# A batch pipeline of SSD mixer and selected-token block: inputs of the next batch normalised inside the scan, gating on one engine, softmax ahead of the decay parts, index sum in bf16

## The chip, the cores and the metric

The kernel runs on 1 core of one Trainium2 chip. The metric is the device time of one launch in microseconds (us). Three runs of the kernel before took 1541.77 to 1546.73 us, median 1543.58 us. One further run was profiled; every row below is from it.

## The reference

Input x is 8 batches of 1024 tokens by 256. Each batch goes through a modulated mixer (a selective state-space scan with 8 heads, state 64, inner width 512) and then a modulated block that works on the 127 tokens with the highest router weights only.

```python
h = _layernorm(x) * (1 + ca) + sa
x = x + ga * mixer(h)
h = _layernorm(x) * (1 + cb) + sb
x = x + gb * block(h)

# mixer
x = silu(causal_conv(h @ Wx.T)); z = h @ Wz.T
b = x @ Wb.T; c = x @ Wc.T; dt = softplus(x @ Wdt.T + b_dt)
state = exp(dt * a) * state + (dt * b) x ;  y = c . state        # per token, per head
y = y + d * x
yn = (y - mean) / sqrt(var + eps) * gn_w + gn_b                  # mean, var over tokens and channels of a head
mixer = (yn * silu(z)) @ Wout.T

# block
weights = h @ router_w + router_b ; sel = sorted indices of the top 127
q, k, v = rope(rmsnorm(h[sel]) @ wq) ... ; a = softmax(q k / 4 + mask[sel, sel])
x1 = h[sel] + (a v) @ wo ; x2 = x1 + gelu(rmsnorm(x1) @ w1) @ w2
block = h for all tokens but sel ; x2 * weights[sel] there
```

## The kernel before

The program is written out by hand: each engine (TensorE = PE, VectorE = DVE, ScalarE = ACT, GpSimd = POOL, SyncE = SP for transfers) has its own list of instructions, works them in order, and waits on semaphores. Nothing reorders them.

PE's `batch(b, f)` interleaves the projections of batch b with the block of batch f = b - 1 and ends with `scan(b)`. So there are 8 passes: batch 0 alone, seven passes with a block of the batch before, and a **tail** in which the block of batch 7 runs alone. A pass on PE goes: transposes of the normalised input (`ln_in`, two halves, line L1509), `x_proj` and `z_proj` (L1521), the output projection of batch f (`out_`, L1685), the projections to B and C (`bc_proj`, L1521), with the steps of the block between them (`ffn_rank` L1708, `ffn_idx` L1718, `ffn_AT` L1790, `ffn_av` L1803 and so on), and the scan.

The scan takes 8 chunks of 128 tokens. For each c PE does: transposes of chunk c+1 (`turn`), decay exponents of c+1 into banks ps0 and ps1 (`cumdiff`), state update (`state`), output of c (`output`, L1588 and L1595), and scores of c+1 into ps2 and ps3 (`scores`, L1636). ACT copies (`tokens`, L775) and takes the exponential (`decay`, L764). DVE does `weigh` (L1094), `state` (L1117), `skip` (L1127, needs the output), `masked` (L1103, needs scores and exponential). The output of the last chunk is computed at the start of the next pass.

The input of batch b+1 (`xin`, a view of tile BT) is loaded during scan b (`prefetch`, L428: once scores of chunk 3 are done, BT's first half is free). DVE then takes its statistics in chunks 4 to 6 (L952 to L969), POOL the reciprocal square root (`ln_in`, L471 to L476), ACT applies it after the scan's last exponential (`ln_apply`, L658), PE transposes it (L1509), ACT copies it out (`ln_rows`, L667). The group norm needs statistics of the whole scan output: `y_stats` (L1134) in two halves, one before and one after the last `skip`, then PE's `gn_stats` (L1673), a short chain over DVE and POOL, ACT's `gn_apply` (L675, 8 pieces), and the gating by silu(z): four pieces on POOL (L582), four on DVE (L1192). PE's `out_` waits for the first half of the gated pieces.

In the block, DVE's `ffn_onehot` writes one-hot matrices `Pm` in fp32 and PE multiplies them by token numbers (L1718) to get the selected indices; DVE converts them, POOL gathers rows and mask rows, DVE normalises (`ffn_norm`). Later DVE's `ffn_scores` scales scores and finds maxima (L1373 to L1379), ACT takes exponentials (L825), DVE divides (`ffn_probs`, L1385 and L1386), PE transposes the result (L1790). `decay_parts` (L1055 to L1070) prepares the decay of batch b for PE's `decay_rows` (L1568).

## Time and profile before

| | |
|---|---|
| median of three runs | 1543.58 us (1541.77 to 1546.73) |
| the profiled run | 1547.94 us, its span from first to last instruction 1546.2 us |
| mean granted clock of PE | 0.959 of full speed |
| PE busy | 1406.5 us, 91% of the span |
| DVE busy | 993.5 us, 64% |
| ACT busy | 693.9 us, 45% |
| POOL busy | 353.1 us, 23% |
| chain that ended last | PE 81%, DVE 10%, issue 4%, ACT 4% |
| one pass, start to start | 1060.55 - 879.79 us = 180.8 us |

The seven passes are alike: the same line begins at the same place in each, 180.8 to 181.1 us apart. The profile is read as follows. Busy times say which engine is nearly full. The waits of PE say how long it stood, for whom, and how often. The timeline, given for one pass (the scan that ends near 1065 us and the pass after it), shows what each engine does at that place. A dash of words in brackets, as in [2.39 <-ACT BT L658], is the idle time of that engine just before the row and what ended it.

### The profile page before, as it was taken

Reading aid. Unit: us, or ns where it says so; the run is one execution under the profiler, and the core shown is the slowest. Engines: PE = TensorE matmul, PEld = TensorE weight load, DVE = VectorE, ACT = ScalarE, POOL = GpSimd, SP = SyncE. Lnnn points to the kernel's source line nnn. Section 1 sums busy time; section 2 is a strip of 40 time slices with the busy share of each in tenths; the row PEclk is TensorE's granted clock in tenths of the full one; section 3 lists DMA queues with packets and bytes.
Section 4 is the critical chain, followed back from the end, with each engine's and each line's share of the span. In section 5 each row is a group of like instructions: output and inputs, shape, how many; then the busy total and the mean of one; then the engine's idle time right before and its main releaser. Section 6 shows DMA issues by size and latency. Waiting matters only on the chain.

```text
span 1546.2 us, 23272 instructions
## 1 busy us (share of the span) xinstructions
PE 1406.5 (91%) x8720; PEld 881.4 (57%) x8720; DVE 993.5 (64%) x2776; ACT 693.9 (45%) x1353; POOL 353.1 (23%) x417
## 2 busy tenths in 40 slices
PE   7999999999999999999999999999999999998444
PEld 2447645675457655576446764576555765466333
DVE  2426787377864787377973778647873679737672
ACT  4443544545354552635445353445526354452212
POOL 3004310332104301143103321043111430033210
PEclk9999999999999999999999999999999999999767
DMA  8000010020002001020010200020010200101010
GB/s 292 1 1 29 21 31 22 4 70 28 25 21 73 1 28 38 7 74 20 19 35 3 71 28 25 21 72 2 28 31 14 73 15 15 44 3 44 28 45 4
DMA packets 47536, 54.26 MB, mean 35 GB/s; under 512 B 7608, under 2 KB 42296, under 8 KB 47424
## 3 DMA queue, kind: packets, MB, share of 16 engines
q1 hardware_dynamic: 41408, 46.42, 9.2%
q0 software_dynamic: 6016, 6.35, 1.6%
q8 instruction: 70, 1.15, 0.3%
q14 instruction: 42, 0.34, 0.1%
HBM read 34.84 MB, written 17.87 MB: 34 GB/s over the span
## 4 chain that ended last, share of the span: by engine, by line
PE 81%; DVE 10%; issue 4%; ACT 4%; POOL 1%; DMA 1%; POOLq 0%; DVEq 0%; SPq 0%; ACTq 0%
PE ps L1521 38%; PE ps L1685 7%; PE ps L1595 4%; PE ps L1588 4%; PE ps L1636 3%; PE ps L1825 2%; PE ps L1648 2%; PE ps L1607 2%; PE ps L1835 2%; DVE xT L1192 2%; PE ps L1622 2%; PE ps L1790 2%; PE ps L1613 1%; PE ps L1509 1%; DVE EC L1373 1%
## 5 line engine op out<-in xcount | busy, mean ns | idle before, releaser
L1521 PE MATMUL ps<-xT,wc_s 128*128 128x512 f32 x512 | 232.6, 609 | 0.0
L1521 PE MATMUL ps<-xT,wb_s 128*128 128x512 f32 x512 | 230.9, 597 | 0.1
L1521 PEld LDWEIGHTS ps<-xT,wc_s 128*128 128x128 f32 x512 | 99.7, 198 | 116.5 <-issue 116.2
L1521 PEld LDWEIGHTS ps<-xT,wb_s 128*128 128x128 f32 x512 | 93.6, 190 | 108.4 <-issue 100.9
L1015 DVE SCALAR_TENSOR_TENSOR xT<-xc,cols_s,xT 128x512 f32<-128x512 f32 x192 | 134.9, 749 | 3.2 <-ACT xT L702 0.6
L1685 PE MATMUL ps<-CT,xT 128*128 128x256 f32 x512 | 114.5, 385 | 16.3 <-DVE xT L1192 16.3
L1685 PEld LDWEIGHTS ps<-CT,xT 128*128 128x128 f32 x512 | 98.1, 193 | 35.3 <-issue 21.9
L1521 PE MATMUL ps<-hT,wx_s 128*128 128x512 f32 x256 | 116.4, 604 | 1.3 <-ACT hT L667 1.3
L1521 PE MATMUL ps<-hT,wz_s 128*128 128x512 f32 x256 | 112.3, 592 | 0.0
L734 ACT ACTIVATE BT<-ps 128x512 f32<-128x512 f32 x64 | 37.9, 592 | 155.8 <-PE ps L1521 155.8
L775 ACT ACTIVATE XB<-ps 128x512 f32<-128x512 f32 x64 | 38.4, 599 | 153.6 <-PE ps L1607 153.6
L734 ACT ACTIVATE CT<-ps 128x512 f32<-128x512 f32 x64 | 38.1, 595 | 142.6 <-PE ps L1521 140.8
L608 POOL TENSOR_TENSOR sm<-sm,mhalf 128x1 f32<-128x1 f32 x24 | 14.4, 599 | 370.3 <-DVE sm L1399 340.2
L764 ACT ACTIVATE Eg<-ps 128x512 f32<-128x512 f32 x128 | 72.3, 596 | 51.8 <-PE ps L1626 47.5
L1117 DVE TENSOR_TENSOR Sbd<-ps,Sdc 64x256 f32<-64x256 f32 x96 | 40.5, 422 | 80.8 <-PE ps L1595 80.2
L550 POOL TENSOR_TENSOR Sdc<-Sbd,dec 128x512 f32<-128x512 f32 x48 | 50.4, 1050 | 143.6 <-DVE Sbd L1117 92.7
L1103 DVE TENSOR_TENSOR Mt<-ps,Eg 128x512 f32<-128x512 f32 x128 | 82.1, 683 | 0.0
L544 POOL TENSOR_TENSOR EC<-EC,CT 128x512 f32<-128x512 f32 x64 | 79.7, 1271 | 1.4 <-POOL dec L535 0.2
L1521 PEld LDWEIGHTS ps<-hT,wz_s 128*128 128x128 f32 x256 | 48.1, 190 | 54.9 <-issue 54.5
L1521 PEld LDWEIGHTS ps<-hT,wx_s 128*128 128x128 f32 x256 | 47.5, 193 | 53.8 <-issue 53.5
L1636 PE MATMUL ps<-CT,BT 64*128 64x128 f32 x1024 | 74.4, 285 | 1.6 <-ACT EC L754 1.6
L1127 DVE SCALAR_TENSOR_TENSOR xT<-xT,cols_s,ps 128x128 f32<-128x128 f32 x256 | 71.9, 343 | 3.8 <-PE ps L1595 1.9
(297 smaller groups left out, 2625.0 us busy)
## 6 DMA issues: line engine op xcount, KB each, us to landing
BT<-x SPq DMA_DIRECT2D x8, 1024.0 KB, 6.7
xr<-x SPq DMA_DIRECT2D x8, 1024.0 KB, 7.5
x_scratch<-xr SPq DMA_DIRECT2D x32, 256.0 KB, 2.1
out<-EC SPq DMA_DIRECT2D x32, 256.0 KB, 2.1
modrow<-mod_scratch SPq DMA_DIRECT2D x8, 512.0 KB, 4.5
w_s<-w SPq DMA_DIRECT2D x2, 1024.0 KB, 11.6
xT<-wmod SPq DMA_DIRECT2D x1, 1024.0 KB, 8.6
wb_s<-wbT SPq DMA_DIRECT2D x1, 1024.0 KB, 11.4
```

Of the source, the lines that this page charges most:

```text
L544: g.tensor_tensor(s, s, CT[:, half, k, :], ALU.mult).then_inc(CE_ready, 1)
L550: g.tensor_tensor(Sdc[:, :, :], Sbd[:, :, :], dec[:, :, c:c + 1].broadcast_to([P, KC, P]), ALU.mult).then_inc(Sdc_ready, 1)
L734: a.activation((BT if m < KC else CT)[:, half, m % KC, :], proj.bank(q)[:, :], ACT.Copy).then_inc(proj.drained[q % 4], 1)
L764: a.activation(Eg[:, s * HALF:(s + 1) * HALF], ps[s][:, :], ACT.Exp).then_inc(Eg_ready, 1)
L1015: ins = v.scalar_tensor_tensor(dst, xcv[:, m, half * HALF + tap:half * HALF + tap + HALF], cols_s[:, m, tap:tap + 1], dst, ALU.mult, ALU.add)
L1103: v.tensor_tensor(Mt[:, c % 2, s * HALF:(s + 1) * HALF], ps[2 + s][:, :], Eg[:, s * HALF:(s + 1) * HALF], ALU.mult).then_inc(Mt_ready, 1)
L1127: ins = v.scalar_tensor_tensor(s, s, cols_s[:, k, 5:6], ps[4][:, k * P:(k + 1) * P], ALU.mult, ALU.add)
L1521: ins = t_.matmul(bank[:, :], w[:, k, m * P:(m + 1) * P], rhs[:, k, half * HALF:(half + 1) * HALF], start=k == 0, stop=k == nk - 1)
L1588: t_.matmul(ps[4][:, k * P:(k + 1) * P], Sbd[:, k, :], ECv[:, k, c * P:(c + 1) * P], start=k == 0, stop=True, skip_group_check=k > 0)
L1595: ins = t_.matmul(ps[4][64 * hh:64 * hh + 64, k * P:(k + 1) * P], XB[:, c % 2, 0, h * STATE:(h + 1) * STATE], Mt[:, c % 2, hh * HALF + k * ...
L1636: ins = t_.matmul(ps[2 + s][:, k * P:(k + 1) * P], BT[r, c // 4, k, chunk(c)], CT[r, c // 4, k, chunk(c)], start=True, stop=True)
L1685: ins = t_.matmul(ps[4 + j][:, i * D:(i + 1) * D], xT[:, k, t * P:(t + 1) * P], wog_s[:, k, :], start=k == 0, stop=k == KC - 1)
```

## The change

What it does, engine by engine:

- SP: in passes 1 to 6 `prefetch(b)` comes ahead of `loads(b)`.
- DVE, scan: the statistics of the next input move one chunk earlier (all of half 0 after `masked` of chunk 4, which is the slot c = 3). `y_stats` has three parts instead of two: chunks 0 to 3, 4 to 6, and 7 alone.
- POOL: `ln_in(b+1, 0)` in slot 4 instead of 6; the product `wog_s` (modulated output weights) moves from slot 4 to behind the scan; no gating.
- ACT: `ln_apply(b+1, 0)` moves ahead of the last chunk's `tokens` and `decay`; transposed probabilities are copied ahead of `w_exp`.
- PE: `ln_in(b+1, 0)` moves into the scan, between the output of chunk 6 and the scores of chunk 7; the first `x_proj` moves ahead of the output of chunk 7. Two bank numbers of the `proj` ring are exchanged for this.
- DVE, gating: all eight pieces.
- DVE, block: the clamp of the mask rows comes after the normalised rows; `ffn_probs` comes ahead of `decay_parts`; the index arrives as two columns (row within the tile, tile number) and is put together by one more instruction.
- PE, index sum: weights are the upper bf16 halves of the fp32 one-hots (every second bf16 element), against a bf16 table with two columns.

```diff
 SP
             for b in range(1, NB - 1):
+                prefetch(b)
                 loads(b)
-                prefetch(b)
                 stores(b)
 POOL
-            link(g.iota(tok[:, :], pattern=[[P, T]], base=0, channel_multiplier=1,
+            link(g.iota(tok[:, :, 0], pattern=[[0, T]], base=0, channel_multiplier=1,
+            link(g.iota(tok[:, :, 1], pattern=[[1, T]], base=0, channel_multiplier=0,
...
-                    if c == 4:
-                        pool.wait_ge(modrow_loaded, at(modrow_loaded, b, 16))
-                        pool.wait_ge(sc_filled, at(sc_filled, b, 8))
-                        g.tensor_tensor(wog_s, ...)
-                    if c == T - 2 and not last:
+                    if c == 4 and not last:
                         ln_in(b + 1, 0)
                 if not last:
                     ln_in(b + 1, 1)
+                pool.wait_ge(modrow_loaded, at(modrow_loaded, b, 16))
+                pool.wait_ge(sc_filled, at(sc_filled, b, 8))
+                g.tensor_tensor(wog_s, ...)
...
-                for half in range(2):
-                    for k in range(2):
-                        pool.wait_ge(yn_ready, at(yn_ready, b, half * KC + k + 1))
-                        g.tensor_tensor(xT[:, k, s], xT[:, k, s], zs[:, k, s], ALU.mult).then_inc(g_ready, 1)
 ACT
                 for c in range(1, T):
+                    if c == T - 1 and not last:
+                        ln_apply(b + 1, 0)
                     tokens(c)
                     decay(c)
                 if not last:
-                    ln_apply(b + 1, 0)
                     ln_rows(b + 1, 0)
                     ln_apply(b + 1, 1)
 DVE
-                        y_stats(0)
+                        y_stats(1, 4, 7)
                     skip(c)
...
+                    if c == 3 and not last:
+                        mod_column(b + 1)
+                        ln_stats(b + 1, (0, 1, 2, 3))
+                        ln_var(b + 1, 0)
                     if c == 4 and not last:
-                        mod_column(b + 1)
-                        ln_stats(b + 1, (0, 1))
+                        ln_stats(b + 1, (4, 5))
                     if c == 5 and not last:
-                        ln_stats(b + 1, (2, 3))
-                        ln_var(b + 1, 0)
-                    if c == 6 and not last:
-                        ln_stats(b + 1, (4, 5, 6, 7))
+                        ln_stats(b + 1, (6, 7))
                         ln_var(b + 1, 1)
+                    if c == 6:
+                        y_stats(0, 0, 4)
-                y_stats(1)
+                y_stats(2, 7, 8)
...
-                    for k in (2, 3):
+                    for k in range(KC):
...
-                ins = v.tensor_copy(self_[:, 0:1], bank[:, 0:1])
+                ins = v.tensor_copy(self_[:, 0:2], bank[:, 0:2])
+                chR(dve, b, v.scalar_tensor_tensor(self_[:, 0:1], self_[:, 1:2], float(P), self_[:, 0:1], ...))
...
-                v.tensor_scalar(sm[:, 0:1], sm[:, 9:10], EPS, None, ALU.add).then_inc(fv_ready, 1)
-                dve.wait_ge(m_loaded, at(m_loaded, b, 16))
-                v.tensor_scalar(mrows, mrows, -3e38, None, ALU.max).then_inc(mclamp_ready, 1)
...
                 v.tensor_scalar(hn, hs, sm[:, 3:4], None, ALU.mult).then_inc(hn_ready, 1)
+                dve.wait_ge(m_loaded, at(m_loaded, b, 16))
+                v.tensor_scalar(mrows, mrows, -3e38, None, ALU.max).then_inc(mclamp_ready, 1)
...
+                    ffn_probs(f, range(4))
                 decay_parts(b)
-                if f is not None:
-                    ffn_probs(f)
 PE
                     state(c)
                     output(b, c)
+                    if c == T - 2 and not last:
+                        ln_in(b + 1, 0)
                     scores(c + 1)
...
-                    ins = t_.matmul(bank[:, 0:1], Pm[:, t, :], tok[:, t:t + 1], start=t == 0, stop=t == T - 1)
+                    ins = t_.matmul(bank[:, 0:2], Pmb[:, t, :], tok[:, t, :], start=t == 0, stop=t == T - 1)
...
-                ln_in(b, 0)
+                if f is None:
+                    ln_in(b, 0)
+                x_proj(b, 0, (0,))
                 if f is not None:
                     output(f, T - 1)
-                x_proj(b, 0, (0, 1))
+                x_proj(b, 0, (1,))
                 ln_in(b, 1)
```

Line numbers of the changed program differ by a few. PE at the end of a scan and the start of the next pass, before:

```order
L1595 MATMUL ps<-Mt,XB 64x128 [waits masked_scores_ready,Xd_ready]
L1595 MATMUL ps<-Mt,XB 64x128 x7
L1636 MATMUL ps<-CT,BT 128x128 [waits masked_scores_ready]
L1636 MATMUL ps<-CT,BT 128x128 x7
L1509 MATMUL ps<-ident,BT 128x128 [waits decay_ready,xn_ready,setup_dve,ffn_weights_loaded]
L1509 MATMUL ps<-ident,BT 128x128 x7
L1588 MATMUL ps<-EC,Sbd 128x128 [waits CE_ready,state_ready,y_ready]
L1588 MATMUL ps<-EC,Sbd 128x128 x3
L1595 MATMUL ps<-Mt,XB 64x128 [waits masked_scores_ready,Xd_ready]
L1595 MATMUL ps<-Mt,XB 64x128 x7
L1521 MATMUL ps<-hT,wx_s 128x512 [waits proj_drained1]
L1521 MATMUL ps<-hT,wx_s 128x512 x3
```
and in the changed program, from the same output of chunk 6 on:

```order
L1593 MATMUL ps<-Mt,XB 64x128 [waits masked_scores_ready,Xd_ready]
L1593 MATMUL ps<-Mt,XB 64x128 x7
L1507 MATMUL ps<-ident,BT 128x128 [waits xn_ready,decay_ready]
L1507 MATMUL ps<-ident,BT 128x128 x7
L1634 MATMUL ps<-CT,BT 128x128 [waits masked_scores_ready]
L1634 MATMUL ps<-CT,BT 128x128 x7
L1519 MATMUL ps<-hT,wx_s 128x512 [waits proj_drained1,proj_drained0,setup_dve,ffn_weights_loaded]
L1519 MATMUL ps<-hT,wx_s 128x512
L1586 MATMUL ps<-EC,Sbd 128x128 [waits CE_ready,state_ready,y_ready]
L1586 MATMUL ps<-EC,Sbd 128x128 x3
L1593 MATMUL ps<-Mt,XB 64x128 [waits masked_scores_ready,Xd_ready]
L1593 MATMUL ps<-Mt,XB 64x128 x7
```
The transposes of the next input (output from ident and BT) now stand ahead of the scores of chunk 7 (CT, BT), and one projection (hT, wx_s) stands ahead of the output of chunk 7 (Sbd, then Mt).

DVE in the scan, from `masked` of chunk 4 to `weigh` of chunk 5, in the changed program:

```order
L1099 TENSOR_TENSOR Mt<-ps,Eg 128x512 [waits decay_ready,scores_filled] x2
L956 COPY mc<-mcol 128x4 [waits proj_drained1]
L948 BN_STATS st<-BT 128x6 [waits x_loaded]
L948 BN_STATS st<-BT 128x6 x3
L943 COPY spare<-mhalf 128x1 [waits chainA]
L963 BN_AGGR mv<-st 128x2 x4
L965 TENSOR_SCALAR rstd<-mv 128x4 [waits chainA]
L1090 TENSOR_TENSOR XB<-ps,dw 128x512 [waits s_filled,bt_filled]
```
and before, from `masked` of chunk 7 on:

```order
L1103 TENSOR_TENSOR Mt<-ps,Eg 128x512 [waits decay_ready,scores_filled] x2
L952 BN_STATS st<-BT 128x6 [waits x_loaded]
L952 BN_STATS st<-BT 128x6 x3
L947 COPY spare<-mhalf 128x1 [waits chainA]
L967 BN_AGGR mv<-st 128x2 x4
L969 TENSOR_SCALAR rstd<-mv 128x4 [waits chainA]
L1134 BN_STATS yst<-xT 128x6 [waits y_ready]
L1134 BN_STATS yst<-xT 128x6 x3
L1127 SCALAR_TENSOR_TENSOR xT<-xT,cols_s,ps 128x128 [waits y_filled,chainS]
L1127 SCALAR_TENSOR_TENSOR xT<-xT,cols_s,ps 128x128 x3
```
and in the changed program, from the same `masked` on:

```order
L1099 TENSOR_TENSOR Mt<-ps,Eg 128x512 [waits decay_ready,scores_filled] x2
L1130 BN_STATS yst<-xT 128x6 [waits y_ready]
L1130 BN_STATS yst<-xT 128x6 x3
L1130 BN_STATS yst<-xT 128x6 [waits y_ready,chainS]
L1130 BN_STATS yst<-xT 128x6 x3
L1123 SCALAR_TENSOR_TENSOR xT<-xT,cols_s,ps 128x128 [waits y_filled,chainS]
L1123 SCALAR_TENSOR_TENSOR xT<-xT,cols_s,ps 128x128 x3
L1130 BN_STATS yst<-xT 128x6 [waits y_ready]
L1130 BN_STATS yst<-xT 128x6 x3
L943 COPY spare<-mhalf 128x1 [waits chainS]
```
Six rows stand between `masked` of chunk 4 and the next `weigh`, where none stood before, and none of the next input's statistics stand behind `masked` of chunk 7 any more.

DVE around the softmax, before (decay parts, then the divisions):

```order
L1065 TENSOR_TENSOR xc<-xc,Rsrc 128x64 [waits chainD]
L1066 TENSOR_TENSOR xc<-xc,Lsrc 128x64
L1067 CAST Rsrc<-xc 128x8x4x2 [waits chainD]
L1068 CAST Lsrc<-xc 128x8x4x2
L1069 TENSOR_TENSOR Rsrc<-xc,Rsrc 128x8x4x2 [waits chainD]
L1070 TENSOR_TENSOR Lsrc<-xc,Lsrc 128x8x4x2
L1385 RECIPROCAL den<-den 128x4 [waits prob_ready]
L1386 TENSOR_TENSOR EC<-EC,den 128x4x127 [waits chainR]
L1385 RECIPROCAL den<-den 128x4 [waits prob_ready]
L1386 TENSOR_TENSOR EC<-EC,den 128x4x127 [waits chainR]
```
and in the changed program:

```order
L1384 RECIPROCAL den<-den 128x4 [waits prob_ready]
L1385 TENSOR_TENSOR EC<-EC,den 128x4x127 [waits chainR]
L1384 RECIPROCAL den<-den 128x4 [waits prob_ready]
L1385 TENSOR_TENSOR EC<-EC,den 128x4x127 [waits chainR]
L1384 RECIPROCAL den<-den 128x4 [waits prob_ready]
L1385 TENSOR_TENSOR EC<-EC,den 128x4x127 [waits chainR]
L1384 RECIPROCAL den<-den 128x4 [waits prob_ready]
L1385 TENSOR_TENSOR EC<-EC,den 128x4x127 [waits chainR]
L1051 COPY xc<-ps 128x128 [waits proj_filled0]
L1055 TENSOR_TENSOR xc<-xc 128x64 [waits proj_drained0]
L1056 CAST Rsrc<-xc 128x8x4x2
L1058 TENSOR_TENSOR xc<-xc 128x64 [waits log_dt_ready]
```
The eight rows of the division now stand ahead of the copy of the cumulated decay (xc from ps), which frees a PE bank.

## Rows read from the trace of the kernel before

**Rows 1.** Waits of PE over the span: line, what ended it, total us, times, longest.
```profile
PE ps L1790 <- DVE EC L1386: 32.0, 8, 10.2
...
PE ps L1509 <- ACT BT L658: 19.3, 8, 2.6
...
PE ps L1685 <- DVE xT L1192: 16.3, 8, 8.3
```

**Rows 2.** Windows of 1 us: busy us (count) by engine, then PEclk, DMA share, GB/s.
```profile
1062.00:1063.00 1.00, 0.22 (x1) 0.25 (x2) 1.00 (x4) 0.63 (x2) 0.00 (x0) 0.67 0.00 0
...
1174.00:1175.00 1.00, 0.87 (x7) 0.71 (x7) 0.97 (x3) 0.79 (x2) 0.00 (x0) 0.99 0.00 0
...
1178.00:1179.00 1.00, 1.00 (x3) 0.51 (x2) 0.00 (x0) 0.00 (x0) 0.00 (x0) 0.80 0.00 0
```

**Rows 3.** Timeline, end of one scan: start, us, engine, line [idle before <-releaser].
```profile
1055.85 0.60 ACT L775 ACTIVATE XB<-ps 128x512 f32<-128x512 f32 x1 [3.26 <-PE ps L1607]
...
1059.22 1.16 PE L1636 MATMUL ps<-CT,BT 64*128 64x128 f32 x16
...
1060.55 2.08 ACT L658 ACTIVATE BT<-BT,mrs,rstd 128x256 f32<-128x256 f32 x4 [2.37 <-POOL mrs L476]
...
1062.78 1.94 PE L1509 MATMUL ps<-ident,BT 128*128 128x128 f32 x8 [2.39 <-ACT BT L658]
...
1064.55 2.47 DVE L1134 BATCH_NORM_STATS2 yst<-xT 128x6 f32<-128x512 f32 x4
...
1073.25 0.28 PE L1673 MATMUL ps<-pk,halfmean 128*128 128x8 f32 x2
```

**Rows 4.** Page's DMA issues, then the timeline inside the same scan.
```profile
BT<-x SPq DMA_DIRECT2D x8, 1024.0 KB, 6.7
...
1038.51 0.37 SPq L428 DMA_DIRECT2D BT<-x  x1
...
1045.02 1.28 DVE L1103 TENSOR_TENSOR Mt<-ps,Eg 128x512 f32<-128x512 f32 x2
...
1053.04 1.09 PE L1595 MATMUL ps<-Mt,XB 128*64 128x128 f32 x16
```

**Rows 5.** All instructions of line L1192, then the timeline of one gating.
```profile
L1192 DVE TENSOR_TENSOR xT<-xT,zs x32: 676/1722/1760, 174.5 to 1441.9; 128x512 f32<-128x512 f32 x32
...
1077.60 5.74 ACT L675 ACTIVATE xT<-xT,gab 128x512 f32<-128x512 f32 x8
...
1083.36 14.05 PE L1685 MATMUL ps<-CT,xT 128*128 128x256 f32 x64 [1.14 <-DVE xT L1192]
```

**Rows 6.** Timeline of DVE and PE around one batch's softmax.
```profile
1168.98 0.17 DVE L1379 TENSOR_SCALAR mx<-mx 128x4 f32<-128x4 f32 x1
...
1172.19 0.69 DVE L1386 TENSOR_TENSOR EC<-EC,den 128x508 f32<-128x508 f32 x1
...
1173.00 0.69 DVE L1386 TENSOR_TENSOR EC<-EC,den 128x508 f32<-128x508 f32 x1
...
1173.03 3.62 PE L1790 MATMUL ps<-ident,EC 128*127 128x128 f32 x16 [3.06 <-DVE EC L1386]
...
1180.95 1.08 PE L1803 MATMUL ps<-EC,ftmp 127*32 127x128 f32 x32
```

**Rows 7.** Timeline of PE around rank and index sums of one batch.
```profile
1122.43 0.49 PE L1708 MATMUL ps<-ones_b,EC 128*128 128x1 bf16 x14
...
1123.34 3.68 PE L1521 MATMUL ps<-xT,wb_s 128*128 128x512 f32 x8
...
1126.85 1.84 PE L1718 MATMUL ps<-tok,Mt 128*128 128x1 f32 x16
...
1128.56 1.96 PE L1521 MATMUL ps<-xT,wc_s 128*128 128x512 f32 x4
```

**Rows 8.** Timeline of the tail, after the last scan.
```profile
1474.74 3.57 PE L1718 MATMUL ps<-tok,Mt 128*128 128x1 f32 x16 [2.02 <-DVE Mt L1269]
...
1486.18 0.69 DVE L1304 TENSOR_SCALAR Mt<-Mt 128x1024 f32<-128x1024 f32 x1 [2.71 <-DMA Mt<-mask,midx]
```

More of the change, by code:

```diff
@@ L1129, in skip, with y_stats @@
                     ins.then_inc(y_ready, 1)
-                def y_stats(half):
-                    dve.wait_ge(y_ready, at(y_ready, b, 4 * half + 4))
+                def y_stats(part, first, end):
+                    dve.wait_ge(y_ready, at(y_ready, b, end))
                     for k in range(KC):
-                        ins = v.bn_stats(yst[:, k, 6 * half:6 * half + 6], xT[:, k, half * HALF:(half + 1) * HALF])
+                        ins = v.bn_stats(yst[:, k, 6 * part:6 * part + 6], xT[:, k, first * P:end * P])
                     chS(dve, b, ins)
@@ L1599, in output, with scan @@
                 ins.then_inc(y_filled, 1)
-            def scan(b):
+            def scan(b, last):
                 def turn(c):
@@ L1907, in batch @@
                     ffn_w2(f)
-                scan(b)
+                scan(b, b == NB - 1)
             batch(0, None)
```

38 lines of the change are left out of this document (19 added, 19 removed).

## Prediction

> **What bounds the kernel now.** I read the page's shares first: PE is busy 91% of the span and makes up 81% of the chain that ended last, and no other engine passes 64%. So a pass (180.8 us, seven alike) lasts as long as PE's work and PE's stops. Next come PE's waits [rows 1]. Three recur in each pass: for the divided softmax (L1790, 32.0 us in 8), for the normalised input (L1509, 19.3), for the gating (L1685, 16.3). The timelines of the pass after 1060 us give one of each: 3.06 us [rows 6], 2.39 us [rows 3], 1.14 us [rows 5]. Last I read the granted clock by microseconds [rows 2]. It falls from full (2.4 GHz) to half (1.2 GHz) within the microsecond from 1062, after the 2.39 us wait, and again at the end of the one from 1174 (mean still 0.99), shortly after the 3.06 us wait; it is back in the one from 1178 (0.80). So two of the three stops cost more than they show: the transposes behind the first take 1.94 us for eight [rows 3]. After the 1.14 us stop 64 multiplications take 14.05 us, the same 0.22 us each as in the rest of that stretch [rows 5], so a stop of that size took no clock.
>
> **The sum** is made against the profiled execution, 1547.94 us (span 1546.2), which is 4.4 us above the median of 1543.58. I carry the difference over to the median.
>
> **1. Next input normalised in the scan.** Before: scores of chunk 7 start at 1059.22, then the wait, and `gn_stats` starts at 1073.25: 14.03 us [rows 3]. What ACT, DVE and POOL do is now done a chunk earlier, so I follow each.
> DVE: statistics of tiles 0 to 3, means and variance stand after `masked` of chunk 4, which ends at 1046.30 [rows 4]. They take about 2.3 us (an estimate, from 2.47 us for four statistics of twice the width [rows 3], plus three short steps), so `weigh`, `state`, `skip` and `masked` of chunk 5 come up to 0.6 us later than before, since `state` had idled for the output. PE needs that `masked` at 1053.04 [rows 4]; by my count it ends at 1052.6. That is the thinnest cover of this part. If it is gone, PE stands for a few tenths.
> ACT: idle 3.26 us before the copy at 1055.85 [rows 3]; the four pieces of 2.08 us fit there, if POOL has the factors by 1053, and POOL gets its variances at 1048.7. On POOL `ln_in` waits ahead of the decayed state of chunk 5, which comes some 0.9 us later and has four of slack. `wog_s` moved past it is wanted at 1083 only.
> PE: 8 transposes at full clock, 0.9 us, then the scores (1.05), then a projection that must wait for ACT's two copies of the transposes: 0.3 to 0.9 us. Projection 1.72, output of chunk 7 2.1, projection 1.72, transposes 0.9, projection 1.72.
> DVE now limits `gn_stats`: `masked` ends at 1062.75, chunks 0 to 3 take 2.47, chunks 4 to 6 1.85 to 2.47 (by width or as before; taken 2.0, nearer the width), `skip` 1.12, chunk 7 0.6 to 1.2 (taken 1.0), aggregation 1.05. That is 1070.4, where PE arrives at 1069.7. So `gn_stats` starts at 1070.45, not 1073.25: **2.8 us** a pass (2.0 to 3.6), and a new wait of 0.7 us for DVE appears there.
>
> **2. Loads.** The prefetch is issued at 1038.51 [rows 4], the moment its semaphores allow; modrow and xr had been issued 5 us before. So the exchange on SP does not load x earlier. It moves the other two behind it; they are wanted by `wog_s` and the residual 20 and 45 us later: nothing. x lands 6.7 us after issue (median), 1045.2, and is now wanted at 1046.3 instead of 1052: 1.1 us of slack.
>
> **3. Gating.** ACT's pieces come 0.72 us apart (5.74 for 8) from 1077.60 [rows 5]. L1192 took 0.68 us at best and 1.72 in the median; the slow ones run while POOL's two-input multiplications run. Without these I take 0.68, so DVE keeps pace with ACT and the first half is ready at 1077.60 + 4 x 0.72 + 0.05 + 0.72 = 1081.3, where PE came at 1082.22. The wait goes: **1.15 us**. Next late is PE itself. If DVE kept its 1.72, four pieces would end at 1085.2 and it would cost 1.9 us; but no two-input work of POOL is left in that stretch.
>
> **4. Softmax ahead of the decay parts.** Before: PE is free at 1169.97, starts at 1173.03, reaches L1803 at 1180.95 [rows 6]. The last maximum ends at 1169.15; the decay parts filled the 3 us after it. Now the divisions begin there, 0.81 us a group (1173.00 - 1172.19); ACT's four last exponentials are done well before the fourth group's turn. The fourth is ready at 1172.4, PE's transposes end at 1172.95, the projection takes 3.44 at full clock, L1803 starts at 1176.5: **4.45 us** (2.8 if the clock still falls). The projection's bank is freed by the first copy of the decay parts, at 1172.75 now: 0.2 us of cover. The parts themselves end 3.1 us later than the divisions, 1175.5, and `decay_rows` wants them at 1177.5.
>
> **5. Index sum in bf16.** 16 passes of fp32 took 1128.56 - 1126.85 = 1.71 us. The nearest bf16 work with one output column is L1708: 36 in 0.91 us, 0.025 each [rows 7], so 8 take 0.2. Its weights are contiguous, here every second element is read; the far end is no gain. I take 0.35: **1.35 us** (0 to 1.5). It is kept only if what comes behind moves along: PE's next wants of DVE (`hn`, mask) had 2.5 us of slack and `hn` is 1.7 us earlier now. The added DVE instruction (0.2 us) stands in the same slack.
>
> Per pass 2.8 + 1.15 + 4.45 + 1.35 = 9.75, times 7 = 68.3 us.
>
> **6. Tail.** The rest of the tail is one dependent chain. Gating of the first half 2.1 us shorter (5.76 to 3.65 from ACT's first piece). Index sum 3.57 us at half clock [rows 8] to about 0.7: 2.9, less 0.2 for the added instruction. The clamp had held DVE 2.71 us for the mask [rows 8], now the rows are normalised meanwhile: 1.55. More and smaller statistics cost 0.55. Together **5.8 us** (4 to 7). Setup: one more small iota on POOL, which idles there: nothing.
>
> Sum 74 us: 1474 profiled, **1470** as median.
>
> **Rivals.** *A. The clock falls anyway at the softmax.* The transposes there run in bursts of 0.45 us every 0.81 us, so PE is half idle for 2.5 us, and the trace cannot tell whether the fall at 1175 came from the wait or from these bursts. Then only 2.8 us are saved there, 1.65 x 7 = 12 us less: 1482. Against it: the stop is now under 0.4 us at a time, and a single one of 1.14 took no clock. The Trainium skill (TensorE: Matmul & The Clock Gate, Part 4: PE-mode transpose) says that a transpose does not count as PE-busy as a matmul does; by that rule the stretch would count as idle and this rival holds. No row here separates the two.
> *B. x is late.* The transfer now shares its queue with 1.5 MB issued behind it. If they are served in turns, x lands some 3.5 us later, DVE stops 2.4 us in the middle of the scan and PE behind it about 3 a pass: 1470 + 21 = 1491. For it: 1.1 us of slack. Against it: before, x shared with the end of xr, which had gone ahead.
> *C. Index sum and first part give half*, since strided weights load slowly and thin covers break: 1470 + 7 x 2 = 1484.
> *D. Slower.* The transposes in the scan are a new wait in PE's order, with the scores, the state and everything of the pass behind it. It decides once x lands some 13 us late (9.75 us of gain, and the transposes had 4 us to spare): if it were served behind modrow, xr and the pass's scatter, say 17 us, it would cost 16 a pass, 1470 + 7 x 16 = 1582. Nothing in the rows speaks for it but the queue order, which puts x first.
> *E. Nothing moves*, because the passes are bound by another chain that only looks like PE: DVE idles 36% and waits for PE at each of these places; 1540.
>
> **Chances.** Forecast 1460 to 1478: 0.60. A 0.16, B 0.05, C 0.12, D 0.02, E 0.01, more gain than summed (both long stops and all half clock gone, 11.5 a pass: 1458) 0.04. Range 1458 to 1492: it takes in A, B and C and the ends of the terms. 0.3%, about what a measurement of this kernel tells from no change, is 4.6 us: faster 0.96, same 0.02, slower 0.02.
>
> **What would show it.** After: L1509's wait of 2.4 us gone from six or seven passes, a small one at `gn_stats` (L1673) instead; L1685's wait gone but in the tail; L1192 at 0.68 us; L1790's wait near 0 and then three of 0.3 to 0.4; full clock through both stretches; L1718's 8 passes within 0.2 to 0.5 us; passes 171 us apart. Wrong if the clock row shows half after the divisions (A), if the first statistics of the scan wait for a transfer (B), or if passes stay over 175 us.

## The result, and the profile after

The changed kernel took 1470.7 us (median of four runs, 1468.33 to 1475.66) beside 1543.86 us for the kernel before: ratio 0.9524, 95% interval 0.9504 to 0.9544. The prediction was 1470.0, range 1458 to 1492. The run that was profiled took 1468.33 us, its span is 1466.3.

From the page of the kernel after: busy time of each engine, the clock by slices, and the chain that ended last by engine.

```profile
PE 1372.3 (94%) x8656; PEld 849.5 (58%) x8656; DVE 996.5 (68%) x2848; ACT 689.5 (47%) x1353; POOL 308.7 (21%) x386
...
PEclk9999999999999999999999999999999999999767
...
PE 87%; DVE 6%; issue 3%; ACT 1%; DMA 1%; POOL 1%; POOLq 0%; SPq 0%; DVEq 0%; ACTq 0%
```

PE does nearly the same work (64 instructions fewer, all of the index sum) in a span 79.9 us shorter. Its waits after (line, releaser, total us, times, longest):

```profile
PE ps L1789 <- DVE EC L1385: 10.2, 1, 10.2
...
PE ps L1673 <- DVE pk L1174: 7.8, 7, 6.3
PE ps L1684 <- DVE xT L1190: 6.3, 1, 6.3
...
PE ps L1605 <- ACT XB L770: 5.1, 8, 0.6
```

Of the three waits of [rows 1], those of the softmax and of the gating were there eight times and are there once, in the tail; the one for the normalised input is gone but for the first batch. New is a wait at `gn_stats` (L1673): 6.3 us in the tail, 1.5 in the other six together.

The passes start 170.76 us apart (847.40 and 1018.16 for `gn_stats`), where two neighbours of before were 180.83 apart. Counted from one `gn_stats` to the next, the seven passes of before were not quite alike: the first took 181.6 us, and the last, which prepares no next input, 177.4. The timeline of PE, kernel after, through the end of a scan and the following passage (start, us, line, [idle before <-releaser]), with one row of DVE:

```profile
1007.10 1.09 PE L1507 MATMUL ps<-ident,BT 128*128 128x128 f32 x8
1008.13 1.16 PE L1634 MATMUL ps<-CT,BT 64*128 64x128 f32 x16
1009.36 1.98 PE L1519 MATMUL ps<-hT,wx_s 128*128 128x512 f32 x4
...
1018.16 0.39 PE L1673 MATMUL ps<-pk,halfmean 128*128 128x8 f32 x2 [0.26 <-DVE pk L1174]
...
1023.45 2.81 DVE L1190 TENSOR_TENSOR xT<-xT,zs 128x512 f32<-128x512 f32 x4 [2.42 <-ACT xT L670]
...
1027.08 3.19 PE L1684 MATMUL ps<-CT,xT 128*128 128x256 f32 x14
```

The output of chunk 6 ends where the transposes start. From there to `gn_stats` it is 11.06 us (1007.10 to 1018.16); in [rows 3] the same stretch, from the scores at 1059.22 to 1073.25, is 14.03. The transposes (1.09 us for eight) run at full clock and before the scores. From `gn_stats` to the output projection it is 8.92 us; before it was 10.11 (1073.25 in [rows 3], 1083.36 in [rows 5]). DVE multiplies a piece in 0.70 us (2.81 for four), where L1192 had a median of 1.72 [rows 5].

Index sum and softmax in the timeline of PE, kernel after, and windows of 1 us through the softmax (busy us by engine, then granted clock):

```profile
1070.49 0.34 PE L1717 MATMUL ps<-tok,Mt 128*128 128x2 bf16 x8
1070.70 1.53 PE L1519 MATMUL ps<-xT,wc_s 128*128 128x512 f32 x3
...
1108.52 3.60 PE L1519 MATMUL ps<-xT,wc_s 128*128 128x512 f32 x8
1112.24 3.10 PE L1789 MATMUL ps<-ident,EC 128*127 128x128 f32 x16
1115.18 3.60 PE L1519 MATMUL ps<-xT,wc_s 128*128 128x512 f32 x8
1118.71 1.08 PE L1802 MATMUL ps<-EC,ftmp 127*32 127x128 f32 x32
```

```profile
1112.00:1113.00 1.00, 0.79 (x5) 0.52 (x4) 0.95 (x4) 1.00 (x7) 0.00 (x0) 1.00 0.00 0
1113.00:1114.00 1.00, 0.83 (x5) 0.69 (x6) 0.95 (x3) 1.00 (x4) 0.00 (x0) 1.00 0.00 0
1114.00:1115.00 1.00, 0.87 (x7) 0.71 (x8) 0.96 (x5) 1.00 (x3) 0.00 (x0) 1.00 0.00 0
```

The index sum takes 0.21 us of PE's order (1070.49 to 1070.70), before 1.71 [rows 7]. From the projection ahead of the softmax to `ffn_av` (L1802) it is 10.19 us; before, the same two rows are 1166.38 and 1180.95, 14.57 apart (the second in [rows 6]). No wait is shown ahead of the transposes, PE is busy 79 to 87% of each microsecond, and the clock stays full. In windows of 1 us over a whole pass (847 to 1019) none is below full.

Loads and tail, kernel after: median of the loads of x from issue to landing; one load's issue and its first use by DVE; then four groups of PE in the tail.

```profile
BT<-x SPq DMA_DIRECT2D x8, 1024.0 KB, 5.5
...
986.38 0.38 SPq L428 DMA_DIRECT2D BT<-x  x1
...
994.16 1.40 DVE L948 BATCH_NORM_STATS2 st<-BT 128x6 f32<-128x256 f32 x4
```

```profile
1366.54 16.18 PE L1684 MATMUL ps<-CT,xT 128*128 128x256 f32 x64 [6.35 <-DVE xT L1190]
...
1400.91 0.37 PE L1717 MATMUL ps<-tok,Mt 128*128 128x2 bf16 x8 [2.02 <-DVE Mt L1267]
...
1411.37 0.69 PE L1725 MATMUL ps<-ident,ftmp 128*128 128x128 f32 x2 [10.09 <-DVE ftmp L1314]
...
1442.94 5.26 PE L1824 MATMUL ps<-ftmp,w_s 128*128 128x128 f32 x32 [0.47 <-ACT ftmp L839]
```

The first statistics of x start 7.8 us after the issue and wait for nothing. In the tail the index sum to the transposes of the normalised rows takes 10.46 us; before 15.30 (1474.74 in [rows 8] to L1726 at 1490.04).

### The profile page after: what moved, and what is told of

It is laid out like the page before. It is cut to its first block, busy times and chain, and to the rows that moved or that the text cites. A ratio compares the mean times of both kernels' runs of the same rounds, so it can differ in the third digit from the quotient of the medians.

```text
span 1466.3 us, 23175 instructions
## 1 busy us (share of the span) xinstructions
PE 1372.3 (94%) x8656; PEld 849.5 (58%) x8656; DVE 996.5 (68%) x2848; ACT 689.5 (47%) x1353; POOL 308.7 (21%) x386
## 3 DMA queue, kind: packets, MB, share of 16 engines
q0 software_dynamic: 6016, 6.35, 1.7%
## 4 chain that ended last, share of the span: by engine, by line
PE 87%; DVE 6%; issue 3%; ACT 1%; DMA 1%; POOL 1%; POOLq 0%; SPq 0%; DVEq 0%; ACTq 0%
PE ps L1519 43%; PE ps L1684 8%; PE ps L1634 5%; PE ps L1593 4%; PE ps L1586 4%; DVE yst L1130 3%; PE ps L1646 2%; PE ps L1605 2%; PE ps L1824 2%; PE ps L1834 2%; PE ps L1620 2%; PE ps L1624 1%; PE ps L1611 1%; PE ps L1789 1%; PE ps L1755 1%
## 5 line engine op out<-in xcount | busy, mean ns | idle before, releaser
L1519 PE MATMUL ps<-xT,wc_s 128*128 128x512 f32 x512 | 225.4, 593 | 0.0
L1519 PEld LDWEIGHTS ps<-xT,wc_s 128*128 128x128 f32 x512 | 96.1, 190 | 112.3 <-issue 111.9
L1519 PEld LDWEIGHTS ps<-xT,wb_s 128*128 128x128 f32 x512 | 93.6, 190 | 108.4 <-issue 100.9
L1406 DVE TENSOR_TENSOR ftmp<-ftmp,ps 128x256 f32<-128x256 f32 x8 | 3.4, 420 | 108.6 <-PE ps L1834 108.6
```

Of the source, the lines that this page charges most:

```text
L1519: ins = t_.matmul(bank[:, :], w[:, k, m * P:(m + 1) * P], rhs[:, k, half * HALF:(half + 1) * HALF], start=k == 0, stop=k == nk - 1)
```

## The experiments

Theory: four parts each take away a stop or a piece of PE's own order in every pass (in sum 9.75 us by the prediction), and the stops cost clock on top. Rivals: the parts hide each other, the clock is lost by the bursts of transposes and not by the stop, x is late. First each part was undone alone in the changed kernel.

### The softmax order undone

```diff
                     ffn_scores(f)
-                    ffn_probs(f, range(4))
                 decay_parts(b)
+                if f is not None:
+                    ffn_probs(f, range(4))
...
-                if f is not None:
-                    ffn_AT(f)
                 w_exp(b)
+                if f is not None:
+                    ffn_AT(f)
```

> The changed kernel with one part undone: the softmax divisions come after the decay parts again (and ACT copies the transposed probabilities after its decay exponential). Theory (each part takes its own stop of PE away, and they add up): PE's wait for the divided softmax is back at about 3.1 us in each of seven passes, the clock falls to half behind it, a pass is 4.4 us longer (171 to 175), 1471 + 31 = 1502 us. Rival (the parts cover each other, PE comes earlier or later and the loss is shared): less than 2.5 us a pass, under 1488 us.

Measured: 1493.61 us (1493.37 to 1494.05), ratio to before 0.9676 (0.965 to 0.9703). A pass takes 174.2 us, 3.4 more than the changed kernel, not 4.4. Waits, timeline of one pass on PE, and windows of 1 us there:

```profile
PE ps L1790 <- DVE EC L1385: 31.6, 8, 10.2
```

```profile
1134.69 3.51 PE L1790 MATMUL ps<-ident,EC 128*127 128x128 f32 x16 [3.06 <-DVE EC L1385]
1138.03 3.60 PE L1520 MATMUL ps<-xT,wc_s 128*128 128x512 f32 x8
```

```profile
1134.00:1135.00 1.00, 0.31 (x1) 0.34 (x2) 0.97 (x3) 0.00 (x0) 0.00 (x0) 0.70 0.00 0
1135.00:1136.00 1.00, 1.00 (x6) 1.00 (x6) 0.97 (x3) 0.09 (x1) 0.00 (x0) 0.50 0.00 0
1136.00:1137.00 1.00, 1.00 (x7) 1.00 (x7) 0.94 (x3) 0.74 (x2) 0.00 (x0) 0.50 0.00 0
1137.00:1138.00 1.00, 1.00 (x7) 1.00 (x7) 0.00 (x0) 0.74 (x2) 0.00 (x0) 0.59 0.00 0
1138.00:1139.00 1.00, 1.00 (x5) 0.52 (x5) 0.00 (x0) 0.81 (x2) 0.00 (x0) 1.00 0.00 0
```

The stop is the same 3.06 us as in [rows 6]. But the clock fell some 0.3 us before its end (a mean of 0.70 from 1134 on) and was back near 1137.8, while PE was still on the transposes; the projection behind them ran at full clock (3.60 us for eight). In the kernel before it fell late, at the end of the microsecond from 1174 [rows 2], and the projection paid (4.57 us for the same eight, from 1176.44). So the stop's own price is 3.1 us, and the clock adds 0.3 or 1.3 by where the stretch at half clock falls. The pass lost 1 us less than the theory had, and the run ended between the theory and the rival.

### The index sum undone

```diff
-        tok = sb("tok", [P, T, 2], BF16)
+        tok = sb("tok", [P, T])
...
-                    ins = t_.matmul(bank[:, 0:2], Pmb[:, t, :], tok[:, t, :], start=t == 0, stop=t == T - 1)
+                    ins = t_.matmul(bank[:, 0:1], Pm[:, t, :], tok[:, t:t + 1], start=t == 0, stop=t == T - 1)
```

> The changed kernel with the index sum in fp32 again (one column, 16 passes of PE instead of 8). Theory: 1.5 us more in each pass and 2.9 us in the tail, 1471 + 13 = 1484 us. Rival (time that PE saves there it stands waiting for DVE or ACT a little later): under 0.5 us a pass, 1471 + 3 + 3 = 1477 us or less.

Measured: 1485.04 us (1482.21 to 1486.38), ratio 0.9615 (0.9587 to 0.9644); a pass 172.25 us, 1.49 more. The rows of the changed kernel on that line (ns min/median/max) show why the strided read was no cost:

```profile
L1717 PEld LDWEIGHTS ps<-tok,Mt x64: 96/96/116, 216.3 to 1401.1; 128*128 128x128 bf16 x64
```

In the kernel before, a load of the same matrix in fp32 took 192 ns in the median, and there were twice as many. Eight steps now take 0.21 us of the order, 0.026 each, as much as the contiguous 0.025 of L1708 [rows 7], whose weights also load in 96 ns each. The Trainium skill (TensorE: Matmul & The Clock Gate, Weight-path perf modes) gives the fast weight load to 128 weights that are not fp32, with a read pattern "packed or strided"; these rows agree (96 ns strided and contiguous, 192 in fp32).

### The gating undone

```diff
+                for half in range(2):
+                    for k in range(2):
+                        s = slice(half * HALF, (half + 1) * HALF)
+                        pool.wait_ge(yn_ready, at(yn_ready, b, half * KC + k + 1))
+                        g.tensor_tensor(xT[:, k, s], xT[:, k, s], zs[:, k, s], ALU.mult).then_inc(g_ready, 1)
...
-                    for k in range(KC):
+                    for k in (2, 3):
```

> The changed kernel with half of the gating on POOL again. Theory: POOL's multiplications and DVE's block each other (0.7 us becomes 1.7), the first half of the gating comes after PE wants it, a wait of 1.2 us is back in each pass and 2 us in the tail, 1471 + 10 = 1481 us; the clock stays full. Rival (DVE now has a pace that PE is not waiting for, since PE arrives later there): within 3 us of 1471.

Measured: 1483.44 us (1482.66 to 1483.63), ratio 0.9609 (0.9583 to 0.9636); a pass 172.13, 1.37 more. The wait is back as it was in [rows 1], and DVE's pieces are as slow as in [rows 5] (the kernel with the gating undone; waits, then the line's durations in ns):

```profile
PE ps L1691 <- DVE xT L1196: 16.3, 8, 8.3
```

```profile
L1196 DVE TENSOR_TENSOR xT<-xT,zs x32: 678/1722/1759, 173.1 to 1381.6; 128x512 f32<-128x512 f32 x32
```

The same instruction takes 1.72 us beside POOL's two-input multiplications and 0.69 without them. Two engines at once finished later than DVE alone, by the 1.37 us that the pass lost.

### The scan part undone

The next input is again normalised after the scan, the load of x stands again behind modrow and xr, and the statistics of the output are taken in two halves.

```diff
-                    if c == T - 2 and not last:
-                        ln_in(b + 1, 0)
...
+                ln_in(b, 0)
...
-                    if c == 3 and not last:
+                    if c == 4 and not last:
                         mod_column(b + 1)
-                        ln_stats(b + 1, (0, 1, 2, 3))
-                        ln_var(b + 1, 0)
+                        ln_stats(b + 1, (0, 1))
```

> The changed kernel with the first part undone: next input's statistics, normalisation and transposes, the statistics of y, the modulated output weights and the loads stand where they stood before; softmax order, index sum, gating and clamp stay changed. Theory: the 2.4 us wait before the transposes and the half clock behind it are back, 3.0 us a pass, 1471 + 20 = 1491 us. Rival (most of the gain in that stretch came with other parts): under 1.5 us a pass, under 1481 us. By the theory the four undone parts add up to 31 + 13 + 10 + 20 = 74 us, all that was gained; by a theory of shared waits they add up to something else.

Measured: 1489.17 us (1488.24 to 1493.13), ratio 0.9654 (0.9624 to 0.9684); the passes 173.7 to 174.1 us, 3.0 more or a little over, but one of 172.2. The wait for ACT is back:

```profile
PE ps L1507 <- ACT BT L655: 19.3, 8, 2.6
```

The pass of 172.2 us (688.3 to 860.4) has the stop too, but its granted clock stays at 1.00 throughout, and it lost only 1.4 us. So of the 3.0 us of this part about half, 1.6, is clock.

### The clamp undone

```diff
+                dve.wait_ge(m_loaded, at(m_loaded, b, 16))
+                v.tensor_scalar(mrows, mrows, -3e38, None, ALU.max).then_inc(mclamp_ready, 1)
                 dve.wait_ge(fr_ready, at(fr_ready, b, 1))
...
-                dve.wait_ge(m_loaded, at(m_loaded, b, 16))
-                v.tensor_scalar(mrows, mrows, -3e38, None, ALU.max).then_inc(mclamp_ready, 1)
```

> The changed kernel with the clamp of the mask rows back ahead of the normalising of the head-norm rows; all else as in the changed kernel. Theory: the passes stay 170.8 us apart (there the mask rows are long in, and both steps wait for nothing), and only in the tail does DVE stand for the mask's transfer ahead of the rows, so the tail loses the 1.55 us that the prediction gave to this part: 1470.7 + 1.6 = 1472.3 us, 1471 to 1474. Rival: the order of the two steps matters in the passes too, since the rows are wanted sooner there: 0.3 us or more a pass, over 1474. The other rival: the tail's gain behind the index sum came from the index sum alone, and the time stays at 1470.7.

Measured: 1473.33 us (1472.71 to 1474.12), ratio 0.9538 (0.9511 to 0.9566); passes 170.75 us. By time alone this interval overlaps the changed kernel's. The tail's timeline decides:

```profile
1402.75 0.37 PE L1717 MATMUL ps<-tok,Mt 128*128 128x2 bf16 x8 [2.02 <-DVE Mt L1267]
...
1415.00 0.69 PE L1725 MATMUL ps<-ident,ftmp 128*128 128x128 f32 x2 [11.88 <-DVE ftmp L1316]
```

12.25 us from index sum to transposes, against 10.46: the clamp's place is worth 1.79 us, in the tail only. The 10.46 us repeat to 0.01 us in the runs that keep the clamp and the index sum as they are in the changed kernel and have no dummy work (softmax, gating or scan part undone, x behind, earlier statistics, the repeat), so 1.79 stands clear of the tail's spread.

The five parts undone one by one cost 22.9, 14.3, 12.7, 18.5 and 2.6 us over 1470.7, together 71.0 of the 73.2 that all of them gave. They hardly hide each other. Each figure is good to about 1 us only (an estimate): the kernel before took 1542.39 us beside four of these runs, 1544.42 beside the fifth and 1543.86 beside the changed kernel.

### x behind the other loads

In passes 1 to 6 modrow and xr are issued first, at the same moment.

```diff
-                prefetch(b)
+                sp.wait_ge(sc_filled, at(sc_filled, b, 8))
+                sp.wait_ge(bt_filled, at(bt_filled, b, 4))
                 loads(b)
+                prefetch(b)
```

> The changed kernel, but in passes 1 to 6 the modulation row and the residual x of the next pass (together 1.5 MB) are issued at the same moment as the next x and ahead of it on the same queue; the amount of data is the same. It prices the case that x comes late. Theory (a queue serves what is issued first, so x had the queue for itself in the changed kernel): x now lands after the 1.5 MB, some 3.5 us or more later than 6.7 us after its issue, DVE stops at the first statistics of the scan, and PE behind it: a pass 2 to 3 us longer, 1470.7 + 6 x 2.5 = 1486 us, 1480 to 1492. Rival: the transfers of one queue are served side by side, x had already been sharing with the 1.5 MB behind it, and the order of issue is worth nothing: within 3 us of 1470.7, with the first statistics 7.8 us after the issue as before.

Measured: 1494.38 us (1491.77 to 1496.01), ratio 0.9667 (0.9638 to 0.9697): 23.7 us over 1470.7, more than the 1480 to 1492 of the theory. By the trace the six passes lost 1.9, 4.3, 4.1, 2.2, 6.0 and 3.6 us (3.7 in the mean). Landing of the loads of x (two of the eight, for the first two batches, are as before); waits of DVE; then, of the pass that lost most, the issue, the first statistics, what PE did behind them, and a window there:

```profile
BT<-x SPq DMA_DIRECT2D x8, 1024.0 KB, 9.9
```

```profile
DVE st L950 <- DMA BT<-x: 19.6, 6, 4.1
```

```profile
1003.71 0.53 SPq L428 DMA_DIRECT2D BT<-x  x1
```

```profile
1014.79 1.40 DVE L950 BATCH_NORM_STATS2 st<-BT 128x6 f32<-128x256 f32 x4 [4.12 <-DMA BT<-x]
```

```profile
1017.53 1.11 PE L1613 MATMUL ps<-ident,BT 128*128 128x128 f32 x4 [3.02 <-DVE XB L1092]
```

```profile
1017.00:1018.00 1.00, 0.47 (x2) 0.48 (x3) 0.99 (x3) 0.00 (x0) 0.99 (x1) 0.50 0.00 0
```

Behind 1.5 MB x landed 9.6 to 11.1 us after its issue (11.1 in the pass shown), and 5.4 to 6.1 us after it with the 1.5 MB behind it. So the queue served, to a large part, what was issued first, and rival B's mechanism of turns is refuted here. The price of a late x was right in kind, and as a single figure of 3 us it missed the clock: DVE stopped 2.6 to 4.1 us for x and PE 1.5 to 3.0 behind it. In the two passes where PE's stop was 1.53 and 1.86 us the clock stayed full, and they lost 1.9 and 2.2 us; in the four with 1.91 to 3.02 us it fell to half, and they lost 3.6 to 6.0.

### The softmax order alone, on the kernel before

```diff
-                decay_parts(b)
                 if f is not None:
                     ffn_probs(f)
+                decay_parts(b)
```

ACT's order is changed with it, as in the first experiment.

> The kernel before with one edit: the softmax is normalised ahead of the decay parts, on DVE and in ACT's order; the rest as in the kernel before. Theory: the stop of 3.06 us and the half clock behind it both go, as in the changed kernel, and a pass gets 4.4 us shorter: 180.8 to 176.4, and 1542.9 - 31 = 1512 us, 1509 to 1514. The rival comes from the run with this part undone, where a pass lost 3.4 us and not 4.4: if 3.4 is what the stop costs and the fourth microsecond belonged to another part of the change, this run comes to 1542.9 - 24 = 1519 us, 1517 to 1522, and the four parts undone add up to less than the whole for another reason. By the theory the projection behind the softmax takes 3.4 us instead of the 4.5 of the kernel before; by the rival there is a stop or a slower piece left elsewhere.

Measured: 1511.88 us (1511.62 to 1515.62), ratio 0.9794 (0.9763 to 0.9825), 32.5 us less than the 1544.42 beside it, or 4.6 a pass. The difference to the 3.4 of the undoing is the clock, in two ways. In the kernel before, the stretch at half clock hit the projection, in the changed kernel with this part undone it did not: that gives the 4.0 to 4.4 us of some passes. The others gained 5.8 us and more, since there the clock no longer fell at the other stop either. The first four passes are 175.10, 176.67, 175.07 and 177.02 us long. The stop for the normalised input is still in all of them. Two of them in the timeline of PE, each with its window of 1 us:

```profile
683.62 1.06 PE L1509 MATMUL ps<-ident,BT 128*128 128x128 f32 x8 [2.40 <-ACT BT L658]
```

```profile
683.00:684.00 1.00, 0.38 (x4) 0.41 (x5) 1.00 (x3) 0.47 (x1) 0.00 (x0) 1.00 0.00 0
```

```profile
859.04 1.78 PE L1509 MATMUL ps<-ident,BT 128*128 128x128 f32 x8 [2.39 <-ACT BT L658]
```

```profile
859.00:860.00 1.00, 0.96 (x6) 0.99 (x7) 1.00 (x4) 0.00 (x0) 0.00 (x0) 0.61 0.00 0
```

The first stop took no clock, the second did. In 1-us windows the pass of 175.07 us has none below full and the one of 177.02 us four. Three of the six passes with this stop have the fall, three have not. In the kernel before, the pass from 892 us on has both falls, eight windows below full; each of the six has both. So in this profile half of the falls at the other stop are gone with the first stop, and 4.6 is a mean of two cases. What ties the two stops is not shown: with the scan part undone, where the softmax stop is gone as well, the fall stayed in five of six.

### Dummy work in the tail for the clock, and the last scan's statistics earlier

PE stops for DVE and ACT in the tail, and its clock is at half for about 62 of the tail's 107 us (mean 0.71 below). Dummy multiplications of constants, into a bank that nothing reads then, fill PE's stops; separately the first statistics of the last scan move to chunk 4. The changed kernel ran beside them. The run with both edits has 13 dummies ahead of `gn_stats`, not 24, since the statistics end sooner there.

```diff
+            def warm(n):
+                for _ in range(n):
+                    t_.matmul(ps[0][:, :], identb[:, :], causal[:, :, :].rearrange("p a n -> p (a n)"),
+                              start=True, stop=True)
...
+            warm(24)
             gn_stats(f)
+            warm(25)
             out_(f)
```

```diff
-                    if c == 6:
+                    if c == (4 if last else 6):
                         y_stats(0, 0, 4)
```

> The changed kernel with dummy multiplications in the tail alone, of constants into a PSUM bank that nothing reads then: 24, 25, 13, 40, 5, 40, 42 and 7 of them (about 0.22 us each at full clock), ahead of the tail's aggregation, output, decay rows, rank, index sum, head norm, transposed attention and its second layer, at the places where PE stands for DVE. They leave the results untouched and are sized to end before the data come. Theory: the tail's real work then finds the full clock (2.4 GHz) instead of half: the long groups of the tail that started at half take 1 to 2 us less, together 4 to 6 us: 1465 to 1467 us. Rival: the tail is bound by DVE and ACT behind each group, and PE's clock only shortens pieces that wait anyway, or the dummies overshoot the wait and push the real work back by what they give: 1470 to 1474.

> The changed kernel, but in the last scan (which normalises no next input) the first statistics of the output are taken at chunk 4 instead of chunk 6, as the kernel before had it in every scan. Theory: in the last scan DVE has no next input to serve, so it can take 2 to 2.5 us of statistics earlier and the aggregation of the tail starts that much sooner: 1470.7 - 2.4 = 1468.3 us, 1467.5 to 1469.5. Rival: the place makes no difference, since DVE still ends with the masked states and the statistics of the last chunks: within 1 us of the changed kernel.

> Both edits together: the dummy multiplications of the tail and the earlier statistics of the last scan. Theory: they add, since the one shortens DVE's way to the tail and the other PE's pieces in it: 1470.7 - 5 - 2.4 = 1463.3 us, 1461 to 1466. Rival: the dummies ahead of the aggregation were sized for the longer wait and now overshoot it by up to 2 us, which takes back the gain of the statistics: 1465 to 1467.

> The changed kernel once more, unchanged, as the mark for the other runs of this chip and for the spread: 1470.7 us, 1468.3 to 1475.7, passes 170.8 us apart; the runs with the higher mean granted clock are the shorter ones.

One thing to set right: the kernel before took the first statistics of the output in chunk 7, not in chunk 4.

| kernel | median us | lowest to highest | ratio to before |
|---|---|---|---|
| changed kernel again | 1470.1 | 1468.41 to 1474.97 | 0.9519 (0.9503 to 0.9534) |
| dummies in the tail | 1464.9 | 1463.85 to 1466.14 | 0.9487 (0.9473 to 0.9502) |
| earlier statistics | 1469.74 | 1469.03 to 1472.18 | 0.952 (0.9505 to 0.9535) |
| both | 1463.5 | 1462.33 to 1465.32 | 0.948 (0.9465 to 0.9495) |

Two groups of the tail with the dummies, at full clock (the tail's mean is 0.94):

```profile
1366.42 14.05 PE L1684 MATMUL ps<-CT,xT 128*128 128x256 f32 x64 [0.94 <-DVE xT L1190]
...
1440.35 3.84 PE L1824 MATMUL ps<-ftmp,w_s 128*128 128x128 f32 x32 [0.47 <-ACT ftmp L839]
```

Beside the 16.18 and 5.26 us of the changed kernel these are most of the gain: 2.1 and 1.4 us of the 4.2 by the trace (5.2 by the medians). The earlier statistics shorten the last pass by 2.45 us (170.68 to 168.23), as their theory had it, but alone their gain in the median, 0.4 us, is less than the measurement tells and less than was forecast; it was not established by time. The tail's own spread is of that size: it took 108.4 us in this profile, and 106.8 and 110.4 in the two of the changed kernel. Both together beat the changed kernel, with intervals that do not meet. There the 40 dummies ahead of the transposes of the rows overshot (index sum to transposes 11.54 us, not 10.46), so the rival's overshoot came at another place than it named, and cost 1.1 us.

The repeat of the changed kernel shows where its spread lies. Its span was 1472.9 us with clock 0.970, against 1466.3 with 0.977, and its passes were 170.75 or 170.76 us too. `gn_stats` of batch 0 starts at 167.29, not 164.37, and from the last one to the end it takes 110.4 us, not 106.8. Windows over the whole tail and through a part near its end, each time first the repeat, then the first profile (busy us by engine, then clock):

```profile
1362.50:1472.88 110.38, 48.02 (x294) 39.27 (x294) 62.93 (x197) 27.78 (x67) 13.37 (x16) 0.65 0.08 27
```

```profile
1359.59:1466.35 106.76, 44.19 (x294) 36.66 (x294) 62.91 (x197) 27.44 (x67) 13.37 (x16) 0.71 0.09 27
```

```profile
1428.00:1452.00 24.00, 11.17 (x67) 9.21 (x68) 11.98 (x28) 10.68 (x39) 0.54 (x1) 0.52 0.07 23
```

```profile
1425.00:1449.00 24.00, 11.25 (x87) 10.03 (x87) 11.11 (x27) 11.77 (x41) 0.54 (x1) 0.72 0.06 19
```

## Why the prediction was right, step by step

**The bound.** Right. PE's chain share rose from 81 to 87% as its waits went, and no other engine took their place. Up to the last `gn_stats` the program is 71.9 us shorter (1431.51 to 1359.59); some 10.5 of that, seven times 1.50, is the index sum's own work, the rest stops of PE and half clock.

**Scan part**, 2.8 us forecast: 2.97 measured (11.06 against 14.03), 3.0 a pass when undone, of which about half is clock. The new wait at `gn_stats` was 0.26 us and not 0.7: PE came at 10.80 us after the start of the stretch (forecast 10.5) and DVE at 11.06 (forecast 11.2). The thin cover at `masked` of chunk 5 held: PE's output of that chunk shows no wait.

**Loads**, forecast nothing for the exchange on SP, slack 1.1 us: x landed in 5.5 us and not 6.7, with 1.5 MB behind it, so the slack was 2.3. x was issued no earlier, as the prediction held, but it landed sooner, which it had not: in the kernel before, the six loads with modrow and xr ahead landed in 6.0 to 7.1 us, the same six after in 5.4 to 6.1. The undoing of the scan part had the exchange undone with it, and its loads were slow again (up to 7.0); SP's order alone was not run. In time the term stays nothing, since no wait for x shows either way.

**Gating**, 1.15: 1.19 by the trace, 1.37 undone.

**Softmax**, 4.45: 4.38 by the trace, 3.4 undone; done alone 4.6 in the mean, which is 4.0 to 4.4 where the clock still fell at the other stop and 5.8 to 6.5 where it did not. The term is right for the kernel before, and it is the sum of a stop of 3.06 and a clock loss whose size depends on what PE has in hand when the clock is down. The prediction took this loss as fixed.

**Index sum**, 1.35: 1.50. This term was mis-sized: 0.35 us was allowed for the strided read where 0.21 was measured, the price of the contiguous row.

**Tail**, 5.8 us in all (6.35 after the last `gn_stats`): from there to the end 114.7 us became 106.8, 7.9 less. By steps: gating 1.95 (forecast 2.1); index sum to transposes of the rows 4.84 (forecast 2.7 and 1.55), of which 1.79 is the clamp and 3.0 the index sum, 3.57 to 0.37 us less the added instruction, each shown by undoing it (12.25 and 13.46 us against 10.46); the other 1.2 us lies behind these transposes (56.17 to 54.98 us), and went with a clock that was back earlier in this run. The repeat shows that this last part isn't the change's: there the stretch behind the transposes takes 57.6 us and the tail 110.4, only 4.3 less than before. The last pass gained 6.7 us, which is the other three parts less about 0.4 for the smaller statistics (forecast 0.55).

**The carrying over.** The sum of 74 us was made against a profiled run 4.4 us above its median, and the two profiles differ by 79.9. The step that failed is the assumption that such an offset stays: the profiled run after stood 2.4 us below its median. The 6 us that the terms fell short and this offset cancelled in part, and the median came out 0.7 us from the forecast; that closeness is in part luck. By stretches the profiles gained: up to the first `gn_stats` 3.5 us (forecast 2.8, the scan part of the first scan), in the six passes with a next input 61.8 (six times 9.75 is 58.5; measured 10.1 to 10.3 each, and 10.8 in the first), in the last pass 6.7 (6.4), in the tail 7.9 (6.35). Against the repeat's profile the span differs by 73.3, close to both the sum and the medians.

**Rival A** is refuted, and its premise was misread. Each burst of four transposes was taken at 0.45 us out of 0.81; measured, PE is busy 79 to 87% of each microsecond there, without a wait that the profile shows and at full clock, in the changed kernel ([rows 2] already had 0.87 in the one from 1174). The same bursts follow in all seven passes, and the clock falls only where the stop stands ahead of them. So the fall in [rows 2] belongs to the stop. The Trainium skill (TensorE: Matmul & The Clock Gate, Part 4: PE-mode transpose) says that a transpose doesn't count as PE-busy in the same way. These fp32 transposes show the contrary: 3 us of them cost no clock in the changed kernel, and with the softmax order undone the clock rose from half to full near 1137.8, after 3.1 us in which PE had nothing else. Here the measurement decides. **Rival B** is refuted by the trace, and its price was found by making x late: 1.9 to 6.0 us a pass, 3.7 in the mean. **C, D and E** fall with the terms: undone, the scan part, the gating and the index sum give back what they were said to give within 0.25 us a pass, the softmax 1.0 us less.

## What to carry to other kernels

Where one engine is the chain, list its stops in one period, and for each ask what the releasing engine did just before that could have come later; here two reorderings and one engine given up removed 6.3 us of stops in each pass (3.06 + 2.39 + 1.14, less the new 0.26), and no work was saved but the index sum. Count a stop of 2 us or more with the clock that it can cost behind it, from rows of this kernel, and as a range, since the loss depends on what is queued there; falls of the clock at the other stops can come and go with such an edit, so undoing a part and doing it alone need not give the same price (3.4 and 4.6 us here). Compare medians by medians: offsets of one profiled run are no property of the kernel, and the head and tail where PE stops often carry the spread.

## What the runs showed of the hardware

The same stop has two prices. With 2.40 us idle the clock stayed full in one pass of the kernel with the softmax order alone, with 2.39 it fell in the next, which was 2.0 us longer (177.02 and 175.07). A stop of 3.06 us cost 3.4 or 4.4 in all. The length alone doesn't decide: with x late, stops of 1.53 and 1.86 us took no clock and stops of 1.91, 2.48, 2.55 and 3.02 us did; the stop for the normalised input did in three of six passes, in five of six or in all, by what else was changed. Which passes are hit was not explained.

An exact repeat of a kernel differed by 6.6 us in its profile while seven passes stayed within 0.01 us of their length: all of it lay in the first 170 and the last 110 us, and in the tail it went with the granted clock (0.65 against 0.71 over the tail, 0.52 against 0.72 over 24 us of it). These were the longest of five runs and the shortest of four.

Dummy multiplications in PE's stops, 196 of them, made the tail 4.2 us shorter by the trace (106.8 to 102.5). The five runs with them lie within 2.3 us and the five of the repeat within 6.6, but that they narrow the spread is not shown: five runs with earlier statistics and no dummies lie within 3.2 us, and four with the clamp undone within 1.4.

Transposes held the full clock (1.00 through 3 us of them) and regained it (3.1 us of them, with the softmax order undone). A 1 MB load landed in 5.4 to 6.1 us with 1.5 MB issued behind it on its queue, and in 9.6 to 11.1 us with the same 1.5 MB ahead.
